# Scores of four tokens per product, and a softmax transposed by TensorE, in a 32-head attention and feed-forward layer

## The chip, the cores and the metric

The kernel runs on one core of one Trainium2 chip. The metric is device time in microseconds (us) of one launch, lower is better. The kernel before takes 755.46 us (median of three runs, 755.1 to 756.2).

## What is computed

2048 tokens (4 x 512) of width 512, all float32. The attention is over the heads of one token: each token has 32 queries, 32 keys and 32 values of 16 numbers, and a score matrix of 32 x 32. Then comes a gated feed-forward part whose weights are first quantised to 16 levels and back, in blocks of 64. The reference, cut to what matters (the latent product is computed there and used nowhere):

```
q = (x @ wq.T + bq).reshape(B, S, 32, 16)      # k, v alike
scores = einsum('bshd,bstd->bsht', q, k) / sqrt(16)
probs = softmax(scores, axis=-1)
context = einsum('bsht,bstd->bshd', probs, v).reshape(B, S, 512)
x = layernorm(x + context)
dq1, dq2, dq3 = nf4_quant_dequant(w1), nf4_quant_dequant(w2), nf4_quant_dequant(w3)
h = silu(x @ dq1.T) * (x @ dq2.T)              # 1376 wide
x = layernorm(x + h @ dq3.T)
```

## The kernel before

All five engines run programs of their own, written out by hand, which meet at semaphores. There is no scheduler: the order on an engine is the order of its loops, and three tables of numbers (`LV_P`, `LV_A`, `LV_F`) say how much of the quantisation is done at each step. Every product of the projections and of the feed-forward part is three fp32r products of split operands (`three`, lines 950 to 952).

**Three stages.** First the projections: 4 blocks of 512 tokens, 12 products of 128 rows each (index `tau`, 0 to 47). Queries, keys and values go to DRAM (`qk_d`, `v_d`) and come back in another layout. Then the attention: 32 groups (index `G`) of 64 tokens, 4 groups to a half block of 256 tokens (`hb`). Last the feed-forward part, 44 steps. Beside all of it runs the quantisation of w1, w2 and w3: GpSimd normalises a unit, ScalarE makes a "level" of it (line 785, `nf_y`), VectorE takes it up (line 1188, `nf_acc`), 15 levels a unit. ScalarE may be three levels ahead of VectorE.

**A group before.** A half block's queries and keys lie in `q_st` and `k_st` as 4 strips of 32 rows; a strip holds two tokens (16 rows each). The keys are block-diagonal: for the first token's rows the second token's 32 columns are zero. So one product gives the scores of two tokens, 32 rows by 64 columns:

```
rows, n = slice(32 * q, 32 * q + 32), GI // J2 * g + i
t = pe.matmul(ps_s[32 * q:32 * q + 32, G % 2, J2 * H * i:J2 * H * (i + 1)],
              q_st[hb % 2][rows, :, n],
              k_st[hb % 2][rows, :, :, n].rearrange("d j h -> d (j h)"), start=True, stop=True)
```

A group is 32 such products (line 1033) into one bank of PSUM, `ps_s[:, G % 2]`. VectorE takes the maxima (`highest`, line 1213), transposes the probabilities of the group before in blocks of 32 x 32 (`swap`, line 1223), and subtracts the maxima (`shift`, line 1217). ScalarE takes the exponential (`exp`, line 837). TensorE multiplies the transposed probabilities by the values (`values`, line 1050, 16 products of 32 rows and 68 columns; the 17th column of each value block is one, and gives the softmax's sum). ScalarE copies that out (`evacuate`, line 843, `ctmp`), TensorE turns it back (`back`, line 1059), ScalarE files it (`context`, line 852, `ctx`).

**The order in iteration G.** TensorE: scores(G), values(G-2), turns of the context (`ct`, line 973), back(G-3), turns of the normalised rows (`xt`, line 977). VectorE: highest(G), swap(G-1), shift(G), levels, `add_context` (lines 1233 to 1240), moments. ScalarE: one or two levels (`steep`), context, exp(G), evacuate(G-2), normalisation (`norm_1`, line 860). Scores(G) wait until shift(G-2) has read the bank (`s_ssub`). The additions of the context, the moments, the normalisation and the `xt` turns come once per 8 groups, in groups 11 to 16, 19 to 24 and 27 to 32; for the first block the additions start at group 11, and so on.

**SP's queue.** SP issues nearly all loads and stores, in order: per half block 8 loads of queries after the last scores that read the slot, 8 loads of keys, 4 of values, and between them loads and stores of the quantisation and of x1.

**Rooms.** SBUF is full, and the same bytes hold the projections' tensors, then those of the attention, then those of the feed-forward part. The allocation order in the program sets what lies over what, and the waits that guard it follow from that.

## Time and profile before

| | |
|---|---|
| median of 3 runs | 755.46 us (755.1 to 756.2) |
| the profiled execution | 755.57 us, its span 753.8 us |
| busy, share of the span | TensorE 90%, its weight loads 74%, VectorE 78%, ScalarE 63%, GpSimd 14% |
| mean granted clock | 0.949 |
| chain that ended last | TensorE 54%, VectorE 24%, issue 9%, DMA 5%, ScalarE 5% |

The profile is of one execution. PE is TensorE, PEld its weight loads, DVE VectorE, ACT ScalarE, POOL GpSimd, SPq the DMA queue of SP. A timeline row is: start in us, length in us, engine, line, operation, result <- operands, shapes, count, and in brackets the idle time before it and what ended it. Rows of one kind that follow one another are merged, so a row's length runs from the first start to the last end. A matrix product in fp32 leaves two records, a turn (a product with the identity in transpose mode) one. Ends of matrix products are modelled; starts are measured.

### The profile page before, as it was taken

How to read it: one execution, taken by the hardware profiler on the slowest of the kernel's cores; microseconds unless marked ns; L12 is line 12 of the kernel's file. 1: busy time of each engine (PE TensorE's matmuls, PEld its weight loads, DVE VectorE, ACT ScalarE, POOL GpSimd, SP SyncE). 2: the span in 40 equal slices, each digit the busy share in tenths (PEclk: the TensorE clock that was granted, in tenths of full speed). 3: DMA queues.
4: the chain of work that ended last, by engine and by line, in shares of the span. 5: the costliest groups of instructions: out<-in, count | busy, mean ns of one | idle time of the engine just before them, and what ended most of it. 6: DMA issues, size and time to landing. Idle time of an engine off the chain costs nothing.

```text
span 753.8 us, 14539 instructions
## 1 busy us (share of the span) xinstructions
PE 680.4 (90%) x5818; PEld 556.7 (74%) x5818; DVE 590.4 (78%) x810; ACT 475.8 (63%) x652; POOL 108.7 (14%) x98
## 2 busy tenths in 40 slices
PE   4969999998986968758999999999999999999983
PEld 3858878787875857647888788888887888888761
DVE  2458999899997997967978998998778885544386
ACT  2559989886845647458638788886657673342134
POOL 0105411231101010101101121111110201000022
PEclk9989999999997988968999999999999999999995
DMA  9934237765684686728023542013313101330447
GB/s 213 231 113 155 98 125 190 175 175 132 108 126 79 178 145 160 198 83 311 1 113 140 194 116 85 17 56 103 140 33 130 63 1 30 138 117 13 158 121 167
DMA packets 132850, 92.90 MB, mean 123 GB/s; under 512 B 90256, under 2 KB 111760, under 8 KB 131504
## 3 DMA queue, kind: packets, MB, share of 16 engines
q1 hardware_dynamic: 131648, 89.88, 43.3%
q10 hardware_dynamic: 1136, 2.10, 1.2%
q8 instruction: 46, 0.75, 0.4%
q14 instruction: 20, 0.16, 0.1%
HBM read 58.07 MB, written 33.88 MB: 122 GB/s over the span
## 4 chain that ended last, share of the span: by engine, by line
PE 54%; DVE 24%; issue 9%; DMA 5%; ACT 5%; POOL 1%; SPq 0%; DVEq 0%; POOLq 0%; ACTq 0%
DVE nf_acc L1188 12%; PE ps_s L950 8%; PE ps_s L952 8%; PE ps_s L951 8%; PE ps_p L950 7%; PE ps_p L952 7%; PE ps_p L951 7%; DMA queries_keys<-qk_p 2%; PE ps_s L1033 2%; ACT nf_y L785 2%; DVE prob L1217 2%; DVE smax L1213 2%; DMA wst<-in_L_attn_wk 2%; PE ps_p L1059 1%; DVE y_tmp L1236 1%
## 5 line engine op out<-in xcount | busy, mean ns | idle before, releaser
L1188 DVE SCALAR_TENSOR_TENSOR nf_acc<-nf_y,nf_acc 128x1024 f32<-128x1024 f32 (+4 forms) x266 | 316.7, 1191 | 35.5 <-ACT nf_y L785 23.6
L785 ACT ACTIVATE nf_y<-nf_w,bound_b 128x1024 f32<-128x1024 f32 (+4 forms) x285 | 286.6, 1048 | 3.7 <-DVE nf_acc L1188 3.3
L705 POOL TENSOR_TENSOR nf_w<-nf_w,nf_rec 128x1024 f32<-128x1024 f32 (+4 forms) x19 | 44.4, 2336 | 308.5 <-DVE nf_rec L1172 308.5
L1322 DVE TENSOR_TENSOR silu<-silu,ps_s 128x512 f32<-128x512 f32 (+1 forms) x44 | 30.1, 685 | 74.5 <-PE ps_s L952 74.4
L950 PE MATMUL ps_p<-x_hl,w_hl 128*128 128x512 f32 x192 | 78.1, 407 | 8.9 <-DVE w_hl L1206 6.3
L950 PE MATMUL ps_s<-x_hl,f_ha 128*128 128x512 f32 x192 | 75.0, 391 | 1.6 <-DVE f_la L1206 1.6
L952 PE MATMUL ps_p<-x_hl,w_hl 128*128 128x512 f32 x192 | 76.3, 397 | 0.0
L951 PE MATMUL ps_p<-x_hl,w_hl 128*128 128x512 f32 x192 | 76.2, 397 | 0.0
L932 ACT ACTIVATE hid_hl<-silu 128x512 fp32r<-128x512 f32 (+1 forms) x44 | 27.8, 632 | 76.1 <-DVE silu L1322 76.1
L952 PE MATMUL ps_s<-x_hl,f_la 128*128 128x512 f32 x192 | 74.8, 390 | 0.0
L951 PE MATMUL ps_s<-x_hl,f_ha 128*128 128x512 f32 x192 | 74.8, 390 | 0.0
L925 ACT ACTIVATE silu<-ps_s 128x512 f32<-128x512 f32 (+1 forms) x44 | 26.2, 597 | 72.1 <-PE ps_s L952 71.9
L1033 PE MATMUL ps_s<-k_st,q_st 32*32 32x64 f32 x2048 | 66.2, 291 | 2.4 <-issue 2.4
L712 POOL TENSOR_TENSOR nf_acc<-nf_acc,nf_max 128x1024 f32<-128x1024 f32 (+4 forms) x19 | 37.1, 1955 | 211.3 <-DVE nf_acc L1188 211.3
L1033 PEld LDWEIGHTS ps_s<-k_st,q_st 32*32 32x32 f32 x2048 | 58.1, 136 | 8.8 <-issue 8.6
L950 PE MATMUL ps_s<-x_hl,f_hb 128*128 128x512 f32 (+1 forms) x160 | 62.4, 390 | 0.0
L952 PE MATMUL ps_s<-x_hl,f_lb 128*128 128x512 f32 (+1 forms) x160 | 62.4, 390 | 0.0
L951 PE MATMUL ps_s<-x_hl,f_hb 128*128 128x512 f32 (+1 forms) x160 | 62.4, 390 | 0.0
L837 ACT ACTIVATE prob<-prob 128x512 f32<-128x512 f32 x32 | 20.2, 630 | 62.6 <-DVE prob L1217 62.6
L950 PEld LDWEIGHTS ps_p<-x_hl,w_hl 128*128 128x128 f32 x192 | 36.6, 191 | 17.7 <-issue 7.0
L1050 PE MATMUL ps_p<-v_bd,probT 128*32 128x68 f32 x1024 | 37.9, 302 | 8.6 <-DVE probT L1223 4.9
L950 PEld LDWEIGHTS ps_s<-x_hl,f_ha 128*128 128x128 f32 x192 | 36.1, 188 | 9.8 <-issue 2.4
(108 smaller groups left out, 1187.4 us busy)
## 6 DMA issues: line engine op xcount, KB each, us to landing
x_hl<-x_parts SPq DMA_DIRECT2D x10, 2048.0 KB, 8.3
queries_keys<-qk_p SPq DMA_DIRECT2D x32, 256.0 KB, 3.4
x_parts<-x_st SPq DMA_DIRECT2D x16, 512.0 KB, 3.6
nf_w<-in_L_ffn_w SPq DMA_DIRECT2D x24, 256.0 KB, 3.1
dequantised<-nf_acc SPq DMA_DIRECT2D x10, 512.0 KB, 2.7
v_blocks<-v_t SPq DMA_DIRECT2D x16, 256.0 KB, 3.2
k_st<-queries_keys SPq DMA_DIRECT2D x64, 64.0 KB, 3.8
v_bd<-v_blocks SPq DMA_DIRECT2D x32, 128.0 KB, 3.5
```

Of the source, the lines that this page charges most:

```text
L705: pool.tensor_tensor(v, v, nf_rec[0:p, 0:w // QBLOCK].unsqueeze(2).to_broadcast([p, w // QBLOCK, QBLOCK]), ALU.mult).then_inc(s_nnorm, 1)
L712: pool.tensor_tensor(acc, acc, nf_max[0:p, u % 2, 0:w // QBLOCK].unsqueeze(2).to_broadcast([p, w // QBLOCK, QBLOCK]), ALU.mult).then_inc(s ...
L785: act.activation(nf_y[0:p, at % NY, 0:w], nf_w[0:p, u % 2, 0:w], ACT.Identity, bias=bound_b[0:p, i:i + 1], scale=STEEP).then_inc(s_ny, 1)
L925: act.activation(silu[0:rows, s % 2], ps_s[0:rows, 0], ACT.Silu).then_inc(s_silu, 1)
L932: act.activation(hid_hl[0:rows, s % 2, 0], silu[0:rows, s % 2], ACT.Copy).then_inc(s_hh, 1)
L950: pe.matmul(dst, wh, rh, start=start, stop=False)
L951: pe.matmul(dst, wh, rl, start=False, stop=False)
L952: return pe.matmul(dst, wl, rh, start=False, stop=stop)
L1033: t = pe.matmul(ps_s[32 * q:32 * q + 32, G % 2, J2 * H * i:J2 * H * (i + 1)], q_st[hb % 2][rows, :, n], k_st[hb % 2][rows, :, :, n].rearra ...
L1050: t = pe.matmul(ps_p[32 * j:32 * j + 32, G % 2, a * MV:(a + 1) * MV], probT[:, G % 2, i], v_bd[hb % 2][:, :, token], start=True, stop=True)
L1188: dve.scalar_tensor_tensor(out=acc, in0=y, scalar=float(NF4[i + 1]), in1=acc, op0=ALU.min, op1=ALU.max).then_inc(s_nacc, 1)
L1322: dve.tensor_tensor(h, h, ps_s[0:rows, 1], ALU.mult).then_inc(s_hid, 1)
```

## The change

- One product gives the scores of four tokens. `q_st` and `k_st` hold two halves of 64 rows; a half holds four tokens of 16 rows, and the keys have four blocks of 32 columns. Each product has 64 rows, 32 result rows and 128 columns, and a group has 16 of them in place of 32. The loads keep their number and size (16 rows each); their targets and tokens change.
- VectorE's transpose is gone. In its place TensorE turns the probabilities, four turns of 128 x 128 per group (`swap`), into the bank that the scores came from, and ScalarE copies the bank into `probT` (`keys_first`).
- Scores(G) now wait for the copy of group G-2, and shift(G) for the swap of G-2. TensorE's order becomes scores(G), swap(G-1), values(G-2), and so on; ScalarE's: levels, copy of G-1, context, exp(G).
- `k_st` is twice as large, and the rooms are laid out anew. `v_bd` slot 0 now lies on weights that are read until projection 44, so GpSimd clears it there and not at 12, and its load moves on SP's queue from projection step 31 to 46; slot 1 is cleared after the last projection and not after 44. `y_tmp`, the x1 buffers and the split weights change places; the load of the second x1 block waits for the last values.

```diff
@@
-    J2, TN = 2, TI // 2
+    R2, TN = 2, TI // 2
@@
-    FIRST_LOADS = {3 * KC * (NBK - 1) + at: what for at, what in ((-7, "keys 0"), (-5, "values 0"), (-3, "keys 1"),
-                                                                  (1, "queries 0"), (3, "queries 1"))}
+    FIRST_LOADS = {3 * KC * (NBK - 1) + at: what for at, what in ((-7, "keys 0"), (-3, "keys 1"), (1, "queries 0"),
+                                                                  (3, "queries 1"), (10, "values 0"))}
@@
-        k_st = [sb(f"k_st{i}", [P, J2, H, KS], F32, att) for i in range(2)]
+        k_st = [sb(f"k_st{i}", [P, Q4, H, KS], F32, att) for i in range(2)]
@@
-        probT = sb("probT", [P, 2, GI, H], F32, att)
+        probT = sb("probT", [P, 2, Q4, Q4 * H], F32, att)
@@ def load_side
-            (q, j), (b, e) = divmod(a, J2), divmod(hb, 2)
-            rows, t0 = slice(32 * q + D * j, 32 * q + D * j + D), TB * e + TI * q + TN * j
-            home = q_st[hb % 2][rows, :, 0:TN] if i == 0 else k_st[hb % 2][rows, j, :, 0:TN]
+            (r, q), (b, e) = divmod(a, Q4), divmod(hb, 2)
+            rows, t0 = slice(D * a, D * a + D), TB * e + TI * q + TN * r
+            home = q_st[hb % 2][rows, :, 0:TN] if i == 0 else k_st[hb % 2][rows, q, :, 0:TN]
@@ def load_x1
-                    sp.wait_ge(s_probT, GG)
+                    sp.wait_ge(s_pv, GG)
@@ GpSimd
-                if slot == 1:
-
-                    pool.wait_ge(s_proj, VALUES_FREE)
+
+                pool.wait_ge(s_proj, (VALUES_FREE, 3 * KC * NBK)[slot])
...
-                if tau == 3 * KC:
+                if tau == VALUES_FREE:
                     clear(0)
                     ones(0)
@@ ScalarE
+            def keys_first(G):
+                act.wait_ge(s_swap, G + 1)
+                wait(act, s_pv, G - 1)
+                act.activation(probT[:, G % 2], ps_s[:, G % 2].rearrange("p (u k) -> p u k", u=Q4), ACT.Copy
+                               ).then_inc(s_probT, 1)
...
             for G in range(GG):
                 steep(LV_A[G])
+                if G:
+                    keys_first(G - 1)
                 for at in CONTEXT_AT.get(G, []):
                     context(at)
                 exp(G)
...
             context(GG - 4)
+            keys_first(GG - 1)
             evacuate(GG - 2)
@@ TensorE
                 if key in TAIL_S[:2]:
-                    pe.wait_ge(s_ssub, GG)
+                    pe.wait_ge(s_probT, GG)
...
-                wait(pe, s_ssub, G - 1)
-                for i in range(GI // J2):
-                    for q in range(Q4):
-                        rows, n = slice(32 * q, 32 * q + 32), GI // J2 * g + i
-                        t = pe.matmul(ps_s[32 * q:32 * q + 32, G % 2, J2 * H * i:J2 * H * (i + 1)],
-                                      q_st[hb % 2][rows, :, n],
-                                      k_st[hb % 2][rows, :, :, n].rearrange("d j h -> d (j h)"), start=True, stop=True)
+                wait(pe, s_probT, G - 1)
+
+                for i in range(GI):
+                    u, c = divmod(i, 4)
+                    r, n = c % 2, TN // NG * g + 2 * u + c // 2
+                    rows = slice(TI * r, TI * r + TI)
+                    t = pe.matmul(ps_s[32 * c:32 * c + 32, G % 2, P * u:P * u + P], q_st[hb % 2][rows, :, n],
+                                  k_st[hb % 2][rows, :, :, n].rearrange("d q h -> d (q h)"), start=True, stop=True)
                 t.then_inc(s_score, 1)
+
+            def swap(G):
+
+                pe.wait_ge(s_exp, G + 1)
+                for u in range(Q4):
+                    t = pe.transpose(ps_s[:, G % 2, P * u:P * u + P],
+                                     prob[:, G % 2, 4 * u:4 * u + 4].rearrange("p q h -> p (q h)"), ident[:])
+                t.then_inc(s_swap, 1)
...
                 scores(G)
+                if G:
+                    swap(G - 1)
                 if G >= 2:
                     values(G - 2)
@@ VectorE
             def shift(G):
                 dve.wait_ge(s_smax, G + 1)
+                wait(dve, s_swap, G - 1)
...
-            def swap(G):
-                dve.wait_ge(s_exp, G + 1)
-                wait(dve, s_pv, G - 1)
-                dve.transpose(probT[:, G % 2].rearrange("p i h -> p (i h)"),
-                              prob[:, G % 2].rearrange("p i h -> p (i h)")).then_inc(s_probT, 1)
...
                 highest(G)
-                if G:
-                    swap(G - 1)
                 shift(G)
```

The order on TensorE in two successive groups of the attention stage, before (a row is the program's line, the operation, result <- operands, the result's shape and how often it follows itself; `ps_s<-k_st,q_st` are scores, `ps_p<-v_bd,probT` values, `ps_p<-ident,ctmp` the back-turn):

```order
603 L1033 MATMUL ps_s<-k_st,q_st 32x64 x32
604 L1050 MATMUL ps_p<-v_bd,probT 32x68 x16
605 L1059 MATMUL ps_p<-ident,ctmp 68x128 x4
606 L1033 MATMUL ps_s<-k_st,q_st 32x64 x32
607 L1050 MATMUL ps_p<-v_bd,probT 32x68 x16
```

The same place on TensorE with the change (`ps_s<-ident,prob` is the swap):

```order
606 L1044 MATMUL ps_s<-k_st,q_st 32x128 x16
607 L1052 MATMUL ps_s<-ident,prob 128x128 x4
608 L1069 MATMUL ps_p<-v_bd,probT 32x68 x16
609 L1079 MATMUL ps_p<-ident,ctmp 68x128 x4
610 L1044 MATMUL ps_s<-k_st,q_st 32x128 x16
```

Half as many products of twice the columns, and four turns between scores and values.

The order on ScalarE in group 6 and at the start of group 7, before (`nf_y` are levels, `ctx` the filing of the context, `prob<-prob` the exp, `ctmp` the evacuation):

```order
139 L785 ACTIVATE nf_y<-nf_w,bound_b 128x1088 x2
140 L852 ACTIVATE ctx<-ps_p 68x32x2x8
141 L837 ACTIVATE prob<-prob 128x512
142 L843 ACTIVATE ctmp<-ps_p 128x272
143 L785 ACTIVATE nf_y<-nf_w,bound_b 128x1088
```

The same place on ScalarE with the change:

```order
144 L785 ACTIVATE nf_y<-nf_w,bound_b 128x1088 x2
145 L843 ACTIVATE probT<-ps_s 128x512
146 L858 ACTIVATE ctx<-ps_p 68x32x2x8
147 L837 ACTIVATE prob<-prob 128x512
```

The copy into `probT` stands behind the levels and ahead of `ctx` and exp.

## Rows read from the trace of the kernel before

**Rows 1.** Windows, attention stage: stretch; us; busy (count) of PE, PEld, DVE, ACT, POOL; clock.
```profile
169.85:349.40 179.55, 142.81 (x3373) 120.52 (x3373) 154.58 (x240) 107.72 (x170) 15.60 (x15) 0.86 0.65 145
```

**Rows 2.** Timeline of PE, one plain group and the next scores.
```profile
202.86 2.08 PE L1033 MATMUL ps_s<-k_st,q_st 32*32 32x64 f32 x64
204.87 1.17 PE L1050 MATMUL ps_p<-v_bd,probT 128*32 128x68 f32 x32
205.97 0.63 PE L1059 MATMUL ps_p<-ident,ctmp 128*68 128x128 f32 x4
206.53 2.07 PE L1033 MATMUL ps_s<-k_st,q_st 32*32 32x64 f32 x64
```

**Rows 3.** Timeline of DVE in the same group: maxima and shift.
```profile
202.42 0.68 DVE L1213 TENSOR_REDUCE smax<-ps_s 128x16 f32<-128x512 f32 x1
...
203.64 0.65 DVE L1217 TENSOR_TENSOR prob<-ps_s,smax 128x512 f32<-128x512 f32 x1
```

**Rows 4.** Timeline of ACT in the same group: levels, exp, evacuation.
```profile
202.15 2.18 ACT L785 ACTIVATE nf_y<-nf_w,bound_b 128x1024 f32<-128x1024 f32 x2
...
204.70 0.62 ACT L837 ACTIVATE prob<-prob 128x512 f32<-128x512 f32 x1
205.22 0.38 ACT L843 ACTIVATE ctmp<-ps_p 128x272 f32<-128x272 f32 x1
```

**Rows 5.** Timeline of PE, the waits in groups 22 and 23.
```profile
272.48 1.18 PE L1050 MATMUL ps_p<-v_bd,probT 128*32 128x68 f32 x32 [1.83 <-issue]
...
284.92 1.04 PE L1059 MATMUL ps_p<-ident,ctmp 128*68 128x128 f32 x4 [4.29 <-ACT ctx L852]
```

**Rows 6.** Timeline of DVE, maxima of groups 19 and 22.
```profile
258.08 0.69 DVE L1213 TENSOR_REDUCE smax<-ps_s 128x16 f32<-128x512 f32 x1 [0.54 <-PE ps_s L1033]
...
277.56 0.69 DVE L1213 TENSOR_REDUCE smax<-ps_s 128x16 f32<-128x512 f32 x1
```

**Rows 7.** Timeline of PE asked at single moments: starts of bursts, scores, then values.
```profile
203.12 0.53 PE L1033 MATMUL ps_s<-k_st,q_st 32*32 32x64 f32 x11
...
204.28 0.54 PE L1033 MATMUL ps_s<-k_st,q_st 32*32 32x64 f32 x11
...
205.10 0.45 PE L1050 MATMUL ps_p<-v_bd,probT 128*32 128x68 f32 x8
...
205.59 0.45 PE L1050 MATMUL ps_p<-v_bd,probT 128*32 128x68 f32 x8
```

**Rows 8.** Windows, line 1033 alone: us, PE, PEld, then clock, DMA share, GB/s.
```profile
202.86:204.87 2.01, 2.01 (x64) 1.81 (x64) 1.00 0.66 96
244.02:246.02 2.00, 2.00 (x64) 1.81 (x64) 0.50 0.07 30
```

**Rows 9.** Windows, line 977 alone (turns of 128 columns), columns as above.
```profile
247.63:248.60 0.97, 0.97 (x8) 0.80 (x8) 1.00 0.98 341
331.23:333.08 1.85, 1.85 (x8) 1.52 (x8) 0.50 0.00 0
```

**Rows 10.** Timeline of DVE in group 0, where no transpose stands between.
```profile
171.99 0.69 DVE L1213 TENSOR_REDUCE smax<-ps_s 128x16 f32<-128x512 f32 x1 [1.52 <-PE ps_s L1033]
172.71 0.69 DVE L1217 TENSOR_TENSOR prob<-ps_s,smax 128x512 f32<-128x512 f32 x1
```

**Rows 11.** Timeline of PE, start of the attention stage.
```profile
169.85 5.81 PE L1033 MATMUL ps_s<-k_st,q_st 32*32 32x64 f32 x192
...
178.47 2.07 PE L1033 MATMUL ps_s<-k_st,q_st 32*32 32x64 f32 x64
...
185.66 1.18 PE L1050 MATMUL ps_p<-v_bd,probT 128*32 128x68 f32 x32 [1.24 <-DVE probT L1223]
187.18 0.63 PE L1059 MATMUL ps_p<-ident,ctmp 128*68 128x128 f32 x4 [0.34 <-ACT ctmp L843]
```

**Rows 12.** Timeline of ACT, the two levels of group 2.
```profile
178.37 2.28 ACT L785 ACTIVATE nf_y<-nf_w,bound_b 128x1088 f32<-128x1088 f32 x2
```

**Rows 13.** Timeline of PE, scores of group 12.
```profile
217.67 2.07 PE L1033 MATMUL ps_s<-k_st,q_st 32*32 32x64 f32 x64 [2.38 <-issue]
```

More of the change, by code:

```diff
@@ L272, in layer_kernel @@
         wst = sb("wst", [P, 2, KC, E], F32, proj)
[L273 removed]
+        room = sb("room", [P, 2 * Q4 * H * KS - 2 * KC * E], F32, proj)
         w_hl = [sb(f"w_hl{i}", [P, 2, KC, E], F32R, proj) for i in range(3)]
@@ L284, in layer_kernel @@
         prob = sb("prob", [P, 2, GI, H], F32, att)
-        beside = sb("beside", [P, 2 * KC * E - 2 * H * KS - 2 * GI * H], F32, att)
-        k_st = [sb(f"k_st{i}", [P, J2, H, KS], F32, att) for i in range(2)]
+        y_tmp = sb("y_tmp", [P, 7 * Q4 * D], F32, att)
+        beside = sb("beside", [P, 2 * KC * E - 2 * H * KS - 2 * GI * H - 7 * Q4 * D], F32, att)
+        k_st = [sb(f"k_st{i}", [P, Q4, H, KS], F32, att) for i in range(2)]
         v_bd_0 = sb("v_bd_0", [P, MV, VS], F32, att)
         v_bd_1 = sb("v_bd_1", [P, MV, VS], F32, att)
-        probT = sb("probT", [P, 2, GI, H], F32, att)
+        probT = sb("probT", [P, 2, Q4, Q4 * H], F32, att)
         ctx = sb("ctx", [MV, H, P], F32, att)
         ctmp = sb("ctmp", [P, NCT, 4 * MV], F32, att)
-        y_tmp = sb("y_tmp", [P, 7 * Q4 * D], F32, att)
         x1_st = sb("x1_st", [P, 2, 2, BK], F32R, att)
@@ L295, in layer_kernel @@
         att.close()
-        x1_hl1 = sb("x1_hl1", [P, 2, KC, BK], F32R)
+        f1_lb = sb("f1_lb", [P, 2, KC, NJG * P], F32R)
         f1_ha = sb("f1_ha", [P, 2, KC, NJG * P], F32R)
-        spare = sb("spare", [P, 2 * J2 * H * KS - 2 * KC * E], F32)
-        x1_hl0 = sb("x1_hl0", [P, 2, KC, BK], F32R)
+        f3_ha = sb("f3_ha", [P, NJG, E], F32R)
         hid_hl = sb("hid_hl", [P, 2, 2, BK], F32R)
         silu = sb("silu", [P, 2, BK], F32)
+        x1_hl0 = sb("x1_hl0", [P, 2, KC, BK], F32R)
+        x1_hl1 = sb("x1_hl1", [P, 2, KC, BK], F32R)
         f1_hb = sb("f1_hb", [P, 2, KC, NJG * P], F32R)
-        f1_lb = sb("f1_lb", [P, 2, KC, NJG * P], F32R)
+        f3_hb = sb("f3_hb", [P, NJG, E], F32R)
         f3_lb = sb("f3_lb", [P, NJG, E], F32R)
-        f3_hb = sb("f3_hb", [P, NJG, E], F32R)
-        f3_ha = sb("f3_ha", [P, NJG, E], F32R)
+        spare = sb("spare", [P, 848], F32)
         f1_la = sb("f1_la", [P, 2, KC, NJG * P], F32R)
@@ L344, in layer_kernel @@
         s_exp = sem("s_exp")
+        s_swap = sem("s_swap")
         s_probT = sem("s_probT")
@@ L429, in load_side, with load_queries, load_keys @@
         def load_side(eng, i, hb, a):
-            (q, j), (b, e) = divmod(a, J2), divmod(hb, 2)
-            rows, t0 = slice(32 * q + D * j, 32 * q + D * j + D), TB * e + TI * q + TN * j
-            home = q_st[hb % 2][rows, :, 0:TN] if i == 0 else k_st[hb % 2][rows, j, :, 0:TN]
+            (r, q), (b, e) = divmod(a, Q4), divmod(hb, 2)
+            rows, t0 = slice(D * a, D * a + D), TB * e + TI * q + TN * r
+            home = q_st[hb % 2][rows, :, 0:TN] if i == 0 else k_st[hb % 2][rows, q, :, 0:TN]
             eng.dma_start(home, qk_d[i, b].rearrange("(d h) t -> d h t", h=H)[:, :, t0:t0 + TN]
                           ).then_inc((s_ldq, s_ldk)[i][hb % 2], 16)
-        def load_queries(eng, hb, which=range(Q4 * J2)):
+        def load_queries(eng, hb, which=range(R2 * Q4)):
             for a in which:
                 load_side(eng, 0, hb, a)
-        def load_keys(eng, hb, which=range(Q4 * J2)):
+        def load_keys(eng, hb, which=range(R2 * Q4)):
             for a in which:
@@ L749, in _ @@
                     for i in range(2):
-                        pool.memset(k_st[i].rearrange("p j h n -> p (j h n)"), 0.0).then_inc(s_kzero, 1)
+                        pool.memset(k_st[i].rearrange("p q h n -> p (q h n)"), 0.0).then_inc(s_kzero, 1)
                 around(LV_P[tau])
@@ L850, in context @@
                     act.wait_ge(s_tr, TURN[("ct", b - 1, len(HEADS) - 1)] + 1)
-                home = ctx[:, :, TI * e:TI * e + TI].rearrange("m h (j n) -> m h j n", j=J2)
-                act.activation(home[:, :, :, GI // J2 * g:GI // J2 * g + GI // J2],
-                               ps_p[0:MV, 2 + G % 2].rearrange("m (n j h) -> m h j n", j=J2, h=H), ACT.Copy
+                home = ctx[:, :, TI * e:TI * e + TI].rearrange("m h (r n) -> m h r n", r=R2)
+                act.activation(home[:, :, :, TN // NG * g:TN // NG * (g + 1)],
+                               ps_p[0:MV, 2 + G % 2].rearrange("m (r n h) -> m h r n", r=R2, h=H), ACT.Copy
                                ).then_inc(s_ctx, 1)
@@ L1047, in values @@
                 for i in range(GI):
+                    r, m = divmod(i, GI // R2)
                     a, j = divmod(i, 4)
-                    token = TN * (i % J2) + GI // J2 * g + i // J2
-                    t = pe.matmul(ps_p[32 * j:32 * j + 32, G % 2, a * MV:(a + 1) * MV], probT[:, G % 2, i],
-                                  v_bd[hb % 2][:, :, token], start=True, stop=True)
+                    c = 2 * (m % 2) + r
+                    t = pe.matmul(ps_p[32 * j:32 * j + 32, G % 2, a * MV:(a + 1) * MV],
+                                  probT[:, G % 2, m // 2, H * c:H * c + H],
+                                  v_bd[hb % 2][:, :, TN * r + TN // NG * g + m], start=True, stop=True)
                 t.then_inc(s_pv, 1)
@@ L1128, in _ @@
                     turn(key)
+            swap(GG - 1)
             values(GG - 2)
@@ L1281, in _ @@
                     low(key)
-            swap(GG - 1)
             for key in XT_AT.get(GG, []) + TAIL_1:
```

5 lines of the change are left out of this document (2 added, 3 removed).

## The prediction

> **What bounds the kernel now.** I first read the table by stages: the attention stage is the one that the change touches, 179.55 us of the span, and in it TensorE is busy for 142.81 us, VectorE for 154.58 and ScalarE for 107.72, at a mean granted clock of 0.86 [rows 1]. No engine is full, so a mean does not say what an edit is worth; the timeline does. Between 202.86 and 210.19 us TensorE goes from scores to values to back-turn to scores with no idle time, 3.67 us for a group of 64 tokens (202.86 to 206.53) [rows 2]. Such tight stretches are groups 5 to 11, 16 to 22 and 24 to 30: 18 periods in which TensorE's own work sets the pace. In the same period VectorE takes 1.22 us from the start of its maxima to that of its shift, with its transpose between them [rows 3], and has its levels besides; it is nearly full, but waits for TensorE. ScalarE runs through two levels (2.18 us), ctx, exp and evacuation in 3.4 us (202.15 to 205.5) [rows 4]. Elsewhere TensorE waits: 1.83 us and 4.29 us in groups 22 and 23 [rows 5]. There VectorE sets the pace: its maxima come at 258.08 and, three groups later, at 277.56 us, 6.5 us a group, since it adds the context and takes moments as well [rows 6]. The stage is thus a chain that changes hands: TensorE, VectorE, ScalarE (normalisation), TensorE again.
>
> **The scores.** Per group 32 products of 64 columns become 16 of 128. Each product leaves two records, so 64 records of 64 columns become 32 of 128: the same 4096 column-records. What matters is whether a product costs by its number or by its columns. Looked at closely, records start in bursts of four (two products). In scores, ten bursts lie between the starts 203.12 and 204.28: 0.116 us a burst of 64-column records. In values, four bursts lie between 205.10 and 205.59: 0.1225 us a burst of 68-column records [rows 7]. Four columns more cost 6.5 ns, 1.6 ns a column; 64 times that is 0.104 us, nearly the whole burst. The scores go at the same pace when the granted clock is 0.50: 2.00 us for 64 records, against 2.01 at 1.00 [rows 8]. So I take the price as by columns, about 0.01 us a burst and 1.65 ns a column, and as untouched by the clock. A new burst is then 0.01 + 0.21 = 0.22 us, eight of them 1.78, where sixteen old ones were 1.86: **0.09 us less** per group. The other end is a fixed price per burst: 8 x 0.116 = 0.93 us, 0.93 less. That the slope comes from 128 rows in place of 32, and not from the columns, is the doubt left.
>
> **TensorE's new turn (swap).** Four 128-column turns per group. The nearest rows are the back-turn, also four of 128 columns between two tiled products: from its start at 205.97 to the scores at 206.53 is 0.56 us with both hand-overs [rows 2]. Bounds: 0.49 (four at 0.97/8 = 0.12 us, no hand-over) and 0.92 (four at 1.85/8 = 0.23, and 0.44 is the difference), the clock at 1.00 and 0.50 [rows 9]. I take 0.56, because it is the same shape in the same place. A tight group becomes 3.67 - 0.09 + 0.56 = **4.14 us**, 0.47 more.
> The records of those back-turns last near 0.3 us but start every 0.12 or less, so it is the spacing that I charge. The Trainium skill (TensorE: Matmul & The Clock Gate, Part 4: PE-mode transpose) gives some 275 ns for a transpose in a kernel's context; charged one after another, as an estimate from that page, a swap would be 1.1 us, and the result some 10 us later than mine. The trace speaks for overlap.
>
> **What VectorE loses.** Its transpose leaves. From maxima to shift was 1.22 us with the transpose between (202.42 to 203.64) [rows 3], and in group 0, where there is none between, 0.72 us (171.99 to 172.71) [rows 10]. So 0.50 us a group, worth that only where VectorE sets the pace.
>
> **What ScalarE gains.** A copy of 128x512 out of PSUM per group, the size of the exp, which with the evacuation behind it takes 0.52 us start to start (204.70 to 205.22) [rows 4]; I take 0.54. A plain group with two levels is then 3.4 + 0.54 = 3.9 us of ScalarE, and one with a single level 1.1 less: under 4.14, so covered. In group 23 it is not: ScalarE carries the chain from exp over normalisation and a level to ctx, and the copy now stands between level and ctx, since the order has it there. That costs 0.54 us once per eight groups. The copy now also frees the PSUM bank: scores(G+1) wait for the copy of G-1, and behind them swap, values and turns of TensorE are queued. In step, the way round is scores 2.1, maxima and shift 1.4, exp 0.7, up to two levels 2.2, copy 0.7: 7.1 us over two groups, under 8.28. Covered by 1.2 us.
>
> **Memory and loads.** The keys' loads are the same eight per half block. k_st is twice as large, so its clearing on GpSimd doubles, in the projections, where GpSimd has time; nothing. v_bd's first clearing moves behind projection 44, ahead of 48, and its load of four DMAs is issued between the last stores on SP's queue, where it holds up two of them by some 2 us; the first values come later than before by the start's delay below, and I see no wait for it. The second x1 load waits for the last values; it is wanted a whole block of steps later: nothing.
>
> **The sum, as a delay that is carried along.**
> - Start: before, three groups of scores run from 169.85 without a wait [rows 11]. Now scores(2) wait for exp, swap and copy of group 0, and scores(3) for copy 1, which is behind two levels (178.37 to 180.65) [rows 12] and takes 0.54: 181.2 us in place of 178.47, 2.7 late. The waits of 1.24 and 0.34 us for VectorE and the evacuation swallow 1.6 [rows 11]. At group 5: +1.1.
> - Groups 5 to 12: 7 x 0.47 = 3.3 more, but TensorE waits 2.38 us at group 12 for the keys [rows 13], whose loads stand on SP's queue behind a load that follows ScalarE's levels of group 7, two tight groups on (1.1 + 2 x 0.47). Both ways give about +2.1.
> - Groups 12 to 16: TensorE's delay reaches the maxima of group 13 (+1.8, slack taken off), then VectorE twice -0.5, the copy +0.54: +1.3 at group 16.
> - Groups 16 to 24: three tight periods +1.4; then VectorE four times -0.5 and the copy +0.54: again +1.3. The same for 24 to 31. The end of the stage hangs on the x1 stores, with 3 us to spare for the last swap: nothing. The feed-forward part is the same work.
> Sum: **+1.3 us**. The profiled execution took 755.57 us (span 753.8), 0.11 above the median of 755.46; so 756.9 by its own time, and 756.8 us as the median. Below 0.2% (1.5 us) a measurement of this kernel tells nothing from no change.
>
> **Rivals.**
> - *Price per burst, not per column* (chance 0.18). Scores 0.93 us shorter: a tight group 3.30 us by TensorE, 3.4 on average by ScalarE. For it: the number of records halves. Against: rows 7. Start +0.5, groups 5 to 12 -1.0, 12 to 16 -1.0, and twice 3 x -0.2 - 2.0 + 0.54 = -2.1: -5.6, about **750**.
> - *The way round over ScalarE decides* (0.20; slower). The copy of G-1 has to be done before scores(G+1). It decides as soon as VectorE takes up its maxima over 1.2 us late, as it does where a level (1.2) or the adding of context lies ahead of them; then each late us goes into both groups of the round, 0.5 a group over the 18 tight ones: +9, about **765**. For it: VectorE was idle for only 0.54 us before the maxima at 258.08 [rows 6]. Against: it has 0.5 us less to do.
> - *The two row halves do not run beside one another as four strips did* (0.06). A burst of 0.45 us, scores 3.6, a group 5.9: 32 x 2.23 = 71 us less the 36.7 that TensorE idles in the stage [rows 1]: +35, about **790**. The Trainium skill (TensorEngine Tiling, Gotcha 1: PSUM Pressure) says that different row tiles cannot access the same PSUM bank at once; here four strips already write one bank, at the pace of values, which have no row tiles [rows 7], so the trace does not bear it out.
> - *The clock stays low* (0.06). Turns pay for a clock of 0.50, 0.11 us each [rows 9], and there are eight a group instead of four: 18 x 0.9 = +16, about **773**. Against: TensorE has less idle time than before. The Trainium skill (TensorE: Matmul & The Clock Gate, Part 4) says that transposes do not count as busy for the clock gate; by that rule this rival would hold. The stretch of eight turns at 247.63 ran at 1.00 [rows 9], so alone it does not decide.
> - The forecast itself: 0.50.
>
> **How the numbers follow.** The forecast's own range is 752 to 761, from a start that costs 0 to 3 us and three stretches at 0.3 to 0.6 a group. With the first rival below and the second above, 747 to 768 holds what I want. Faster by over 0.2%: the first rival 0.18 and 0.11 of the forecast's lower end, 0.29. Slower: 0.20 + 0.06 + 0.06 and 0.14 of the forecast, 0.46. Between: 0.25.
>
> **What would show it.** Scores of 1.8 to 1.9 us in 32 records, at both clocks; a swap of 0.56 us; plain groups 4.1 us apart; VectorE with idle time before its maxima in plain groups; group 16 about 1 us later than 244.02. Scores near 1.1 us would make me wrong on the fast side; TensorE idle before scores, released by the copy, on the slow side, and so would bursts of 0.45 us.

## The result and the profile after

The changed kernel takes 761.7 us (761.39 to 762.0, four runs) against 755.5 us: a ratio of 1.0083, with a 95% interval of 1.0067 to 1.0099. It is slower by 6.2 us: inside the stated range of 747 to 768, 4.9 us above the forecast of 756.8, and 0.7 us above the range of 752 to 761 that the prediction gave its own forecast. The profiled execution took 761.39 us with a span of 759.5, where before it was 753.8: 5.7 us to explain.

First the table by stages. Windows of the changed kernel: the attention stage, a tight stretch in it, and the projections from the second block's first product on; columns as in [rows 1].

```profile
172.70:352.14 179.44, 156.45 (x2477) 109.84 (x2477) 139.04 (x208) 124.51 (x202) 20.22 (x23) 0.94 0.66 147
196.20:217.34 21.14, 21.14 (x361) 14.01 (x360) 14.76 (x18) 16.80 (x29) 2.01 (x1) 1.00 0.77 142
64.70:172.70 108.00, 104.10 (x465) 85.08 (x465) 99.44 (x86) 94.42 (x108) 32.64 (x14) 0.98 0.52 149
```

The last of them in the kernel before:

```profile
64.30:169.85 105.55, 103.22 (x466) 83.87 (x465) 98.47 (x86) 95.07 (x109) 33.31 (x21) 1.00 0.56 157
```

The attention stage, the only one that the prediction gave a price, is as long as before: 179.44 us against 179.55 [rows 1]. It is made up otherwise, with TensorE up by 13.6 us and VectorE down by 15.5. The projections from the second block on take 108.0 us for 105.55, and the feed-forward part, from 352.14 us to the end, 407.4 for 404.4 (349.40 to 753.8). With 0.4 us ahead of the second block that is 0.4 + 2.45 - 0.1 + 3.0 = 5.75: in this profile **nearly the whole loss lies in the two stages that the prediction called "nothing" and "the same work"**.

Inside the attention stage, the timeline of TensorE in a plain group and at the start of the stage:

```profile
172.70 3.88 PE L1044 MATMUL ps_s<-k_st,q_st 64*32 64x128 f32 x64
...
178.51 2.04 PE L1044 MATMUL ps_s<-k_st,q_st 64*32 64x128 f32 x32 [0.92 <-ACT probT L843]
...
183.53 2.04 PE L1044 MATMUL ps_s<-k_st,q_st 64*32 64x128 f32 x32 [0.90 <-ACT probT L843]
...
204.66 2.05 PE L1044 MATMUL ps_s<-k_st,q_st 64*32 64x128 f32 x32
206.64 0.66 PE L1052 MATMUL ps_s<-ident,prob 128*128 128x128 f32 x4
207.23 1.18 PE L1069 MATMUL ps_p<-v_bd,probT 128*32 128x68 f32 x32
208.34 0.63 PE L1079 MATMUL ps_p<-ident,ctmp 128*68 128x128 f32 x4
208.90 2.05 PE L1044 MATMUL ps_s<-k_st,q_st 64*32 64x128 f32 x32
```

From start to start: scores 1.98 us (2.01 before [rows 2]), swap 0.59, values 1.11, back-turn 0.56; a period of 4.24 by these rows (4.23 as the mean of groups 5 to 11), for 3.67 in [rows 2]. VectorE and ScalarE in a plain group:

```profile
202.54 0.69 DVE L1236 TENSOR_REDUCE smax<-ps_s 128x16 f32<-128x512 f32 x1 [0.21 <-PE ps_s L1044]
203.27 0.69 DVE L1241 TENSOR_TENSOR prob<-ps_s,smax 128x512 f32<-128x512 f32 x1
...
206.77 0.69 DVE L1236 TENSOR_REDUCE smax<-ps_s 128x16 f32<-128x512 f32 x1 [1.62 <-PE ps_s L1044]
```

```profile
203.10 0.60 ACT L843 ACTIVATE probT<-ps_s 128x512 f32<-128x512 f32 x1 [1.26 <-PE ps_s L1052]
203.59 0.58 ACT L858 ACTIVATE ctx<-ps_p 68x512 f32<-68x512 f32 x1
```

Maxima to shift is 0.73 us, where it was 1.22 [rows 3], and both engines now wait for TensorE.

### The profile page after: what moved, and what is told of

Its sections match the earlier page's. It is cut to its first block, busy times and chain, and to the rows that moved or that the text cites. A ratio compares the mean times of both kernels' runs of the same rounds, so it can differ in the third digit from the quotient of the medians.

```text
span 759.5 us, 12777 instructions
## 1 busy us (share of the span) xinstructions
PE 699.1 (92%) x4922; PEld 549.0 (72%) x4922; DVE 575.9 (76%) x778; ACT 492.4 (65%) x684; POOL 111.6 (15%) x98
## 4 chain that ended last, share of the span: by engine, by line
PE 61%; DVE 19%; DMA 6%; issue 6%; ACT 6%; SPq 1%; POOL 1%; POOLq 0%; DVEq 0%; ACTq 0%
PE ps_s L961 9%; PE ps_s L960 9%; DVE nf_acc L1211 9%; PE ps_s L959 9%; PE ps_p L959 7%; PE ps_p L961 6%; PE ps_p L960 6%; PE ps_s L1044 5%; DMA queries_keys<-qk_p 2%; ACT nf_y L785 2%; PE ps_p L1069 2%; PE ps_p L1079 1%; DMA part<-in_L_attn_hidden_states 1%; DVE smax L1236 1%; DVE y_tmp L1254 1%
## 5 line engine op out<-in xcount | busy, mean ns | idle before, releaser
L1044 PE MATMUL ps_s<-k_st,q_st 64*32 64x128 f32 x1024 | 65.2, 406 | 1.8 <-ACT probT L843 1.8
L1044 PEld LDWEIGHTS ps_s<-k_st,q_st 64*32 64x32 f32 x1024 | 37.0, 137 | 20.9 <-issue 5.0
L959 PEld LDWEIGHTS ps_p<-x_hl,w_hl 128*128 128x128 f32 x192 | 37.0, 193 | 19.4 <-issue 9.4
L959 PEld LDWEIGHTS ps_s<-x_hl,f_ha 128*128 128x128 f32 x192 | 36.1, 188 | 10.0 <-issue 2.1
L961 PEld LDWEIGHTS ps_p<-x_hl,w_hl 128*128 128x128 f32 x192 | 36.9, 192 | 8.2
L960 PEld LDWEIGHTS ps_s<-x_hl,f_ha 128*128 128x128 f32 x192 | 36.1, 188 | 9.1 <-issue 0.5
```

Source lines behind the costliest of these rows:

```text
L959: pe.matmul(dst, wh, rh, start=start, stop=False)
L960: pe.matmul(dst, wh, rl, start=False, stop=False)
L961: return pe.matmul(dst, wl, rh, start=False, stop=stop)
L1044: t = pe.matmul(ps_s[32 * c:32 * c + 32, G % 2, P * u:P * u + P], q_st[hb % 2][rows, :, n], k_st[hb % 2][rows, :, :, n].rearrange("d q h - ...
```

## The experiments

Times of different comparisons are set against the kernel before as measured beside them (755.0 to 756.1 us), so the ratios are what to compare. The stages are those of each run's profiled execution: from the second block's first projection product to the first scores, from there to the first feed-forward product, and from there to the start of the last product. Runs 1, 4, 5 to 9 and 11 are edits of the changed kernel, runs 2, 3, 10 and 12 of the kernel before; runs 6, 7 and 8 have the two repairs of run 5 in them.

| kernel | us | ratio (95%) | second block on | attention | feed-forward |
|---|---|---|---|---|---|
| before | 755.5 | | 105.56 | 179.55 | 391.46 |
| change | 761.7 | 1.0083 (1.0067 to 1.0099) | 108.01 | 179.45 | 394.49 |
| 1 low halves in step | 758.47 | 1.0039 (1.0027 to 1.0051) | 108.10 | 179.72 | 391.58 |
| 2 before, out of step | 758.99 | 1.0044 (1.0031 to 1.0057) | 105.70 | 179.13 | 395.96 |
| 3 before, weights in step | 755.63 | 0.9997 (0.9984 to 1.0009) | 105.58 | 179.85 | 394.85 |
| 4 clear early | 759.79 | 1.0056 (1.0044 to 1.0068) | 105.59 | 180.65 | 394.38 |
| 5 = 1 + 4 | 756.93 | 1.0015 (1.0004 to 1.0027) | 105.61 | 180.54 | 391.58 |
| 6 half products | 757.14 | 1.0014 (1.0002 to 1.0026) | 105.61 | 181.56 | 391.56 |
| 7 turn twice | 762.17 | 1.0080 (1.0055 to 1.0105) | 105.61 | 184.18 | 393.51 |
| 8 turn quarter | 752.99 | 0.9953 (0.9941 to 0.9966) | 105.60 | 176.68 | 391.91 |
| 9 = 5, contexts at 14 | 750.68 | 0.9940 (0.9927 to 0.9953) | 105.54 | 173.57 | 391.61 |
| 10 = 3, contexts at 14 | 750.81 | 0.9946 (0.9934 to 0.9958) | 105.59 | 175.04 | 391.88 |
| 11 = 5, copy first | 760.99 | 1.0074 (1.0062 to 1.0086) | 105.62 | 184.86 | 391.44 |
| 12 before, 64 words off | 756.04 | 1.0010 (0.9994 to 1.0026) | 105.70 | 179.31 | 391.38 |

**The feed-forward part: where the rooms lie (1, 2, 3, 12).** The feed-forward weights lie in two sets of rooms that are used in turn, a and b, each with a high and a low half of the split operand (f1_ha and f1_la, f3_ha and f3_la, and b alike; the profile writes f_ha for both of the first kind). Grouped by shape, the change's products with the a rooms, then those with the b rooms, show what is different (mean ns of a record behind the comma):

```profile
L961 PE MATMUL ps_s<-x_hl,f_la 128*128 128x512 f32 x192 | 76.0, 396 | 0.0
L960 PE MATMUL ps_s<-x_hl,f_ha 128*128 128x512 f32 x192 | 75.3, 392 | 0.0
...
L961 PE MATMUL ps_s<-x_hl,f_lb 128*128 128x512 f32 x128 | 49.8, 389 | 0.0
```

The same groups before:

```profile
L952 PE MATMUL ps_s<-x_hl,f_la 128*128 128x512 f32 x192 | 74.8, 390 | 0.0
L951 PE MATMUL ps_s<-x_hl,f_ha 128*128 128x512 f32 x192 | 74.8, 390 | 0.0
```

Records overlap, so the pace is in their starts. Three products (one triple) take 0.69 us in the change and 0.68 before:

```profile
354.30 0.39 PE L959 MATMUL ps_s<-x_hl,f_ha 128*128 128x512 f32 x1
...
354.99 0.39 PE L959 MATMUL ps_s<-x_hl,f_ha 128*128 128x512 f32 x1
```

```profile
449.99 0.39 PE L950 MATMUL ps_s<-x_hl,f_ha 128*128 128x512 f32 x1
...
450.67 0.39 PE L950 MATMUL ps_s<-x_hl,f_ha 128*128 128x512 f32 x1
```

In ns, the starts are 227 apart before, and in the change 228, 229 and 236 within a triple of gate and up and 231 to 232 on the median for down, with the a rooms; with the b rooms they are 227. In the kernel's room list, which the diff above leaves out, the change has a `spare` of 848 words ahead of f1_la. It puts f1_la, f3_la and minus_i behind them 80 words off the 128-word steps on which the other rooms of these products stand.

```
run 1, change:  spare = sb("spare", [P, 848], F32)  ->  [P, 896]
run 2, before:  + off = sb("off", [P, 80], F32)   ahead of f1_la
run 3, before:  room = sb("room", [P, 2 * J2 * H * KS - 2 * KC * E + MV * VS + 112], F32, proj)
run 12, before: as run 2, with 64 for 80
```

Run 1, expected: 

> The changed kernel with 48 words more in spare, so that f1_la and f3_la begin, like all other rooms of the feed-forward part, a whole number of 128-word steps behind x1_hl0 (in the change they are 80 words off such a step). Theory P (place of the operands): in the changed kernel the products of gate and up with the a rooms follow each other in 228, 229 and 236 ns (line 959, 960, 961), those of down in 232, 231 and 231, all of them 227 before the change and with the b rooms; put in step, 192 triples gain 12 ns and 96 triples 13 ns, 3.5 us in the feed-forward part, and the kernel takes 758.2 us instead of 761.7. Theory T (traffic: loads or another engine's writes in the groups that use the a rooms slow them): the pace stays and the time stays at 761.7.

Run 2, expected: 

> The kernel before with a pad of 80 words ahead of f1_la, so that f1_la and f3_la stand as far off a 128-word step as in the changed kernel; nothing else. Theory P: the pace of the products with the a rooms goes from 227 ns to some 231 on average, the feed-forward part gets 3 to 3.5 us longer, 758.5 to 759 us against 755.5. Theory T: 755.5, nothing moves.

Both came as theory P said. In step the changed kernel is 3.2 us faster (758.47), and out of step the kernel before gets the slow records, the same to the nanosecond, and is 3.1 us slower. Run 1:

```profile
L961 PE MATMUL ps_s<-x_hl,f_la 128*128 128x512 f32 x192 | 74.8, 390 | 0.0
```

Run 2:

```profile
L953 PE MATMUL ps_s<-x_hl,f_la 128*128 128x512 f32 x192 | 76.0, 396 | 0.0
L952 PE MATMUL ps_s<-x_hl,f_ha 128*128 128x512 f32 x192 | 75.4, 392 | 0.0
```

Run 12, expected: 

> The kernel before with a pad of 64 words ahead of f1_la, where 80 words made the products with the a rooms follow each other in 230 to 234 ns instead of 227 and the kernel take 758.99 us. 16 and 80 words off a 128-word step are slow so far, 0 is not. If a 64-word step is enough for the operands: 227 ns and 755.0 to 755.9 us. If it takes the whole 128 words: 230 to 234 ns and 758.5 to 759 us.

A step of 64 words (256 bytes) is enough: the starts are 227 ns apart again, and the kernel takes 756.04 us. Offsets of 16 and 80 words, which are both 16 off a 64-word step, are slow.

```profile
L953 PE MATMUL ps_s<-x_hl,f_la 128*128 128x512 f32 x192 | 74.8, 390 | 0.0
```

Run 3, expected: 

> The kernel before with 112 words more in room, so that the projections' weights (w_hl) stand in step with both blocks' inputs (before, w_hl is 16 words off x_hl_0 and in step with x_hl_1). In the kernel before the products of blocks 0 and 2 follow each other in 233 ns, those of blocks 1 and 3 in 227 to 230. Theory P: blocks 0 and 2 come down to 227 to 229, 288 products by 5 ns, 1.4 us off the projection stage where TensorE is the bound there, some 1 us where VectorE is; 754.1 to 754.5 us. Theory T: 755.5.

The pace came as expected, the time did not. In the kernel before the products of blocks 0 and 2 (counted from 0) started every 233 ns, those of 1 and 3 every 227 to 228; w_hl stands 16 words off x_hl_0 and in step with x_hl_1. With w_hl moved, blocks 0 and 2 went at 228 to 229 ns on average and the others stayed. So it is the **place of the two operands to one another** that counts, not that of one alone. The few products of f_ha and f_hb with minus_i in the feed-forward part say the same: f_ha and f_hb are in step with everything else in all these kernels, but where minus_i is 80 words off (the change and run 2) their starts are 233 ns apart, and 226 to 227 in the kernel before and in runs 1 and 12. How the loss is shared out within a triple is open: with only the low half out of step, the two products of the high half, in step themselves, also come 1 to 3 ns later. In run 3 the stage from the second block on took 105.58 us, as before: TensorE's wait for VectorE's x_hl took the gain up, 3.3 us in three waits for 2.3 in two. What TensorE gains ahead of a wait for VectorE is not gained. The changed kernel has its projection weights in step as well, and goes at 227 to 229 ns in all blocks.

**The projections: the clear of k_st (4, 5).** The prediction had the doubled clear on GpSimd in time that GpSimd has to spare. GpSimd had it to spare, but VectorE had not. GpSimd, then VectorE, in the change:

```profile
85.49 7.85 POOL L750 MEMSET k_st<- 128x4608 f32 x2
```

```profile
92.27 1.62 DVE L1207 TENSOR_SCALAR nf_acc<-nf_y 128x1024 f32<-128x1024 f32 x1
```

and the clear and the same level before, where the clear had ended at 88.98:

```profile
84.98 4.00 POOL L750 MEMSET k_st<- 128x2304 f32 x2
```

```profile
91.76 0.69 DVE L1184 TENSOR_SCALAR nf_acc<-nf_y 128x1024 f32<-128x1024 f32 x1
```

The level of 0.69 us takes 1.62: it starts at 92.27, the clear ends at 93.34 (85.49 + 7.85), and the level ends 0.55 us behind that. The scalar_tensor_tensor levels beside the clear keep their 1.2 us. The Trainium skill (SBUF — State Buffer, Who interferes with whom) says that a tensor_scalar can take a second pair of ports, which VectorE shares with GpSimd under an exclusive lock, and that whichever comes second waits for the whole of the other's instruction. The trace agrees within 0.14 us: 93.34 - 92.27 + 0.69 = 1.76 us by that rule, 1.62 measured. VectorE is busy for 41.8 of the 44.7 us from 64.30 to 109.00 in the kernel before, so the delay reaches TensorE:

```profile
101.87 0.47 PE L959 MATMUL ps_p<-x_hl,w_hl 128*128 128x512 f32 x1 [2.36 <-DVE x_hl L1229]
```

It was 1.31 us at this place before. Behind the idle time of 2.36 us, about 1 us after the products start again, the granted clock falls to its lower level (1.2 GHz, 0.50 in the row). Windows of the change:

```profile
102.00:104.00 2.00, 2.00 (x8) 1.55 (x9) 1.90 (x2) 0.67 (x1) 0.00 (x0) 0.76 0.14 49
104.00:106.00 2.00, 2.00 (x6) 1.62 (x5) 2.00 (x3) 0.00 (x0) 0.00 (x0) 0.50 0.00 0
106.00:108.00 2.00, 2.00 (x9) 1.59 (x9) 0.54 (x2) 1.63 (x3) 0.00 (x0) 0.89 0.04 13
```

Run 4, in the change, GpSimd's program:

```
             normalise(0)
+            pool.memset(k_st[1]...).then_inc(s_kzero, 1)
...
-                    for i in range(2):
-                        pool.memset(k_st[i]...).then_inc(s_kzero, 1)
+                    pool.memset(k_st[0]...).then_inc(s_kzero, 1)
```

Expected: 

> The changed kernel with the second key room cleared by GpSimd right after its first normalise, at about 24 us, instead of beside the first one at 85 us, where the two clears take 7.85 us together (4.00 before the change) and end over VectorE's first level of the next weight unit, which takes 1.62 us for 0.69. Theory C (the clear costs): that level goes back to 0.7 us, TensorE's wait for x_hl at 99.5 us falls from 2.36 to about 1.3 us, the granted clock does not fall to 0.50 behind it (102 to 106 us), and the projection stage ends 2 to 2.5 us sooner: 759.2 to 759.7 us. Rival N: the wait is there for another reason (the stage's later start), the clear is hidden, and the time stays at 761.7.

It came as theory C said. In its trace the level takes 0.69 us, and TensorE waits 1.44:

```profile
92.62 0.69 DVE L1207 TENSOR_SCALAR nf_acc<-nf_y 128x1024 f32<-128x1024 f32 x1
```

```profile
101.30 0.47 PE L959 MATMUL ps_p<-x_hl,w_hl 128*128 128x512 f32 x1 [1.44 <-DVE x_hl L1229]
```

In its windows from 102 to 108 us the clock is 1.00 and TensorE has 33 records for 23 (8 + 6 + 9 in the rows above). The stage is 105.59 us, the loss of 2.4 gone. Of it, 0.92 us is TensorE's shorter wait. The rest goes with the clock: in the change nine products take 3.65 us (102.87 to 106.52), and at 227 ns each they would take 2.04, 1.6 less. The attention stage is 1.1 to 1.2 us longer in runs 4 and 5 than in the change, so a part is given back. In run 4 that is there by the last scores, in run 5 it comes mostly behind them, and run 1, which keeps the late clear, has 0.3 of it. The cause was not tried, and part of it may be the difference between executions.

Run 5, expected: 

> Both repairs of the changed kernel together: the low halves in step with the other rooms (758.47 us alone) and the early clear (759.79 alone), against 761.7 of the change. The two lie in different stages, so they should add: 761.7 - 3.2 - 1.9 = 756.6 us; the projection stage 152.2 us from its first product (154.8 in the change), the attention stage 179.4 to 180.7, the feed-forward part 391.5. That would be the whole loss apart from about 1 us at the start. If either repair only moved the wait elsewhere: 758 us or more.

The two add up. 756.93 us is 1.0015 of the kernel before (1.0004 to 1.0027): **what the change does apart from the two losses costs about 1.1 us**, 0.3 to 2.0 by the interval, near the +1.3 that the prediction gave it.

**The price of the scores (6).** The body of scores in run 6:

```
for v in range(2):
    for i in range(GI):
        ...
        t = pe.matmul(ps_s[32 * c:32 * c + 32, G % 2, P * u + TI * v:P * u + TI * v + TI], q_st[hb % 2][rows, :, n],
                      k_st[hb % 2][rows, 2 * v:2 * v + 2, :, n]..., start=True, stop=True)
```

Expected: 

> On top of the two repairs: every scores product of 128 columns issued as two of 64 (32 a group instead of 16, the same 2,048 columns a group, the four column tiles still taken in turn). Theory L (price by columns, the one of the prediction): a group's scores keep their 2.0 us, the attention stage stays within 1 us, the time within 1 us of the kernel with the two repairs (756.6). Rival N (price by product, 0.116 us for each burst of four records, whatever its width): before the change 64 columns cost 0.116, so two bursts would still take 0.23 us and nothing could be told; but if what is paid has a part per product, the scores get longer by that part. What tells: two bursts of 64 columns against one of 128 (0.24 us of 4 records each way). Equal within 0.01 us: only columns count in this range. A part of 0.02 us per burst: scores + 0.16 us a group, 3 us over the tight groups.

```profile
197.70 2.09 PE L1045 MATMUL ps_s<-k_st,q_st 64*32 64x64 f32 x64
199.72 0.66 PE L1055 MATMUL ps_s<-ident,prob 128*128 128x128 f32 x4
```

The scores take 2.02 us from start to start for 64 records of 64 columns, and 1.98 for 32 of 128: eight bursts more cost 0.04 us, 5 ns each. Theory L holds. The attention stage is 1.0 us longer, as 32 x 0.04 = 1.3 would have it, and the time, 757.14, cannot be told from run 5's 756.93. With 32 rows in place of 64 it took 2.01 us before, so the number of rows does not count either.

**What TensorE's turn is worth (7, 8).** The four turns issued twice (`for u in 2 * list(range(Q4))`), and one turn of four (`range(1)`). Run 8 leaves out the turn of three quarters of the probabilities, so the products behind it work on unturned numbers and the output is not the layer's.

Run 7, expected: 

> On top of the two repairs: the four turns of a group issued twice. They cost 0.58 us from the swap's start to the next one's, so TensorE has some 0.45 to 0.58 us more a group. Theory B (TensorE is the bound in the 18 tight groups alone; in the others ScalarE and VectorE have slack to give): 18 x 0.5 = 9 us on the attention stage, 765 to 766 us. Rival E (TensorE bound in every group now): 32 x 0.5 = 16 us, 772 us. Rival S (the slack covers it): under 3 us, below 760.

Run 8, expected: 

> On top of the two repairs: one of a group's four turns is left, the other three columns of the bank are copied as they stand (keys and probabilities left unturned: that part of the output is left out). TensorE has 0.35 to 0.44 us less a group. Theory B: the tight groups give it back in full, 18 x 0.4 = 7 us off the attention stage, 749 to 750 us; the groups with turns, levels or the context's wait give nothing. Rival S (VectorE or ScalarE bound right behind TensorE): the group's period falls by less than half of it and the time stays above 753.

TensorE in run 7, then in run 8:

```profile
196.66 1.09 PE L1052 MATMUL ps_s<-ident,prob 128*128 128x128 f32 x8
...
201.32 1.09 PE L1052 MATMUL ps_s<-ident,prob 128*128 128x128 f32 x8
```

```profile
198.89 0.33 PE L1052 MATMUL ps_s<-ident,prob 128*128 128x128 f32 x1
...
202.79 0.33 PE L1052 MATMUL ps_s<-ident,prob 128*128 128x128 f32 x1
```

The tight period goes to 4.66 and to 3.90 us, in full as theory B has it. But against run 5's 4.23 us the stage of run 7 should have been 18 x 0.43 = 7.7 us longer, and was 3.6 longer; that of run 8 should have been 18 x 0.33 = 5.9 shorter, and was 3.9 shorter. (Another 1.9 us of run 7's profile lie in the feed-forward part, which the edit does not touch.) Every theory's time missed both runs: 762.17 us lies below B's 765, 752.99 above its 750. Most of what is missing shows up where ScalarE has the lead, in the wait of TensorE's back-turn (line 1079) for ctx: it shrinks by 3.0 us when the tight groups get longer and grows by 2.5 when they get shorter. Run 7, run 5 and run 8 (us in total, times, the longest):

```profile
PE ps_p L1079 <- ACT ctx L858: 8.7, 3, 3.0
```

```profile
PE ps_p L1079 <- ACT ctx L858: 11.7, 6, 3.5
```

```profile
PE ps_p L1079 <- ACT ctx L858: 14.2, 6, 3.8
```

**The wait that caps the stage (9, 10).** In run 5, ScalarE idles 3.7 us before exp(14). Then come norm_1 (2.92 us), a level, and only then two context copies, for the first of which TensorE's back-turn of group 12 waits 3.4 us. The edit, for b = 0 to 2, on run 5's kernel (run 9) and on run 3's (run 10):

```
- LATE = {8 * b + 8 + k: 8 * b + 14 + k // 2 for ...}
+ LATE = {8 * b + 8 + k: 8 * b + 14 for ...}
```

Run 9, expected: 

> The changed kernel with the two repairs (756.93 us), and in LATE all four held-back context copies go to group 8b+14 instead of two to 14 and two to 15; neither kernel's order had this. ScalarE idles 3.7 us before exp(14) (233.8 to 237.5 us), and TensorE's turn of group 12's values waits 3.4 us at 240 us, three times, for two context copies that stand behind norm_1 (2.92), a level and a copy. Theory V (these waits bound the stage, which is why half of what the turns cost or give does not come through): 3 x 2 to 3 us off the attention stage, 748 to 751 us. Rival W (VectorE's moments or ScalarE's norm_1, which the next turns of block b wait for, hold the same place): under 1 us a block, 754 us or more.

Run 10, expected: 

> The kernel before with its weights in step (755.63 us) and the same move of two context copies to group 8b+14. There TensorE waits 4.8 us at 236.6 us and 4.3 us at 284.9. Theory V: 3 x 2.5 to 3.5 us off, 745 to 748 us, and the kernel beats both; it then also stands ahead of the changed kernel with the same move by some 3 us, since that one's tight groups are TensorE's. Rival W: 753 us or more.

Both beat both kernels: 750.68 and 750.81 us, 0.6 and 0.5% under the kernel before. They also equal one another, where 3 us in favour of the kernel before was expected: with the contexts at 14, the change costs nothing that can be measured. Run 9, waits of TensorE in the attention stage:

```profile
PE ps_s L1052 <- ACT prob L837: 5.6, 7, 1.7
...
PE ps_p L1079 <- ACT ctx L858: 1.3, 3, 0.7
```

The wait of 11.7 us has become 1.3 and the stage is 7.0 us shorter, as theory V has it. In run 10 the stage is 4.8 us shorter than in run 3, and my expectation of 745 to 748 missed. There the wait for ctx (18.4 us in the kernel before) is 4.1, but TensorE's turns now wait for norm_1 itself:

```profile
PE ps_t L977 <- ACT part L860: 6.4, 3, 2.2
...
PE ps_p L1059 <- ACT ctx L852: 4.1, 3, 1.9
```

**ScalarE's order (11).** `keys_first(G - 1)` ahead of `steep(LV_A[G])`, on run 5's kernel. Expected: 

> The changed kernel with the two repairs (756.93 us), and ScalarE copies the turned probabilities ahead of the group's levels instead of behind them. TensorE waited for that copy 2.2 us in the whole stage, 3 times. Theory B (TensorE's own work bounds the tight groups): at most these 2 us come back, 755 to 757 us. The prediction's rival (ScalarE's way round decides): 2 us or more in each of several blocks, below 753. A third way: the levels come later by 0.5 to 2 us and VectorE waits for them, 758 us or more.

The third way came true: 760.99 us. TensorE's wait for the copy falls from 2.2 to 0.7 us, but now VectorE waits for its levels, 20.2 us in 21 waits, where it was 7.7 in 4 in run 5:

```profile
DVE nf_acc L1211 <- ACT nf_y L785: 20.2, 21, 2.8
```

## Why the prediction was right and where it was wrong

The range held, and the direction was the likeliest of the three, but the number is luck. What I forecast was +1.3 us, and the rivals that widened the range up to 768 did not come true. Of the 6.2 us measured, some 5 came from two steps that I put at nothing, and they merely fell within that room. The account of the attention stage, the part that I did work out, is right in the main. Point by point:

- *"The feed-forward part is the same work."* This step failed. The work is the same, but the rooms are not: the loss is 3.0 us by the stages, 3.2 by run 1 and 3.1 by run 2. I had read the room list for overlaps alone.
- *"k_st is twice as large, so its clearing on GpSimd doubles ...; nothing."* This step failed too: the loss is 2.45 us in the stage and 1.9 in run 4's time. I asked whether GpSimd had time, not whom it locks out, nor what a wait of TensorE's costs in clock behind it.
- *The scores, 0.09 us less.* The mechanism was right, by columns and not by bursts (1.98 us for half the bursts, and run 6), but they gave 0.03. The term was mis-sized. Inside a group five bursts of the change take 1.15 us, so one is 0.23 and not 0.22:

```profile
204.91 0.63 PE L1044 MATMUL ps_s<-k_st,q_st 64*32 64x128 f32 x5
...
206.06 0.63 PE L1044 MATMUL ps_s<-k_st,q_st 64*32 64x128 f32 x5
```

  Against the 0.116 us of 64 columns [rows 7] that is nearly 1.8 ns a column. I had taken 1.65, from two kinds of product that differ by only four columns.
- *The swap, 0.56 us.* It took 0.59. The tight group is 4.23 us where I had 4.14, which is +0.56 for +0.47.
- *VectorE 0.50 less, ScalarE's copy 0.54 more.* Measured are 1.22 - 0.73 = 0.49, and 0.49 for the copy (203.10 to 203.59). Both were right. So was the way in which they enter: VectorE's maxima of groups 19 and 22, before at 258.08 and 277.56 [rows 6], are

```profile
263.37 0.69 DVE L1236 TENSOR_REDUCE smax<-ps_s 128x16 f32<-128x512 f32 x1 [1.67 <-PE ps_s L1044]
...
281.46 0.68 DVE L1236 TENSOR_REDUCE smax<-ps_s 128x16 f32<-128x512 f32 x1
```

  Counted from the stage's start, their delay is 2.4, 2.0, 1.5, 1.1 and 0.6 us in groups 19 to 23 and 1.0 in group 24: four times 0.5 less, then the copy.
- *The start and the way on.* Scores(3) came 2.2 us late, counted from the stage's start (183.53 - 172.70 against 178.47 - 169.85), where I had 2.7. At group 12 the delay was 222.66 - 172.70 - (217.67 - 169.85) = 2.1, as forecast, and the 2.38 us wait for the keys [rows 13] was gone. At group 16 it was 0.8 for 1.3, at group 24 1.1 for 1.3.
- *The end of the stage, +1.3.* It was -0.1 in the change's profile, +0.2 in run 1's, and +1.0 and +1.1 in those of runs 5 and 4. Two of these are near the forecast; why the other two are not stays open.
- The rivals. *Price per burst*: refuted by the scores' 1.98 us, where it would have some 1.1, and by run 6. *The way round over ScalarE*: TensorE waited 1.8 us for the copy in the change, not 9; run 11 shows that ScalarE's order does hold something, VectorE's levels. *Row halves*: a burst takes 0.23 us, not 0.45. The rule of the Trainium skill on row tiles in one bank (TensorEngine Tiling, Gotcha 1: PSUM Pressure) would have had them one behind another, and no such wait shows. *The clock stays low*: it was 1.00 from 196.20 to 217.34 us with eight turns a group, and 0.94 over the stage for 0.86. By the Trainium skill's rule that turns do not count as busy for the clock (TensorE: Matmul & The Clock Gate, Part 4) this rival was to hold, and it did not. The rule itself is not settled by that, since products fill the other 3.1 us of each group.
- The 18 tight groups are no price list: by runs 7 and 8 only about half to two thirds of a tight group's change reaches the end, since TensorE's wait for ScalarE's late context copies takes up the rest. The sum for the stage still came near run 5's +1.0, because I carried the delay from stretch to stretch instead of multiplying it.

## What to carry to other kernels

When a change moves rooms, every product and every clear that touches a moved room is part of the change: list the offsets of both operands of the hottest products, and see who works beside a clear that got longer. When an edit of a tight stretch pays only in part, look for the next wait after it, since that one may be the cheaper thing to mend: here moving two copies per block gave 5 to 6 us in either kernel, and the change itself gave nothing.
